# A chained transformer kernel on Trainium2: value products of the softmax attention issued for two key steps at a time

## What is computed

```python
def _L1_attn_ref(embedded, Wq, bq, Wk, bk, Wv, bv, gamma, beta):
    B, S, D, H = (2, 256, 128, 16)
    ...
    qk = jnp.einsum('bhqd,bhkd->bhqk', q, k)
    ...
    qk = qk / jnp.float32(np.sqrt(s))
    p = jax.nn.softmax(qk, axis=-1)
    ...
    mask = jnp.triu(jnp.ones((s, s), dtype=p.dtype), k=0)
    p = p * mask
    z = jnp.einsum('bhqk,bhkd->bhqd', p, v)
    ...
    x = embedded + z
```

## Time and profile before

| | us |
|---|---|
| median of 3 runs | 970.51 |
| lowest, highest | 967.36, 974.08 |
| the profiled execution | 969.55 |
| its span in the trace | 967.8 |

### The profile page before, as it was taken

How to read it: one execution, slowest core, us unless ns; L and a number is a source line. 1 busy time by engine, 2 the same in 40 slices (tenths; PEclk the granted TensorE clock), 3 DMA queues, 4 the chain that set the end, 5 groups by cost and what they waited for, 6 DMA issues and landing times.

```text
span 967.8 us, 13758 instructions
## 1 busy us (share of the span) xinstructions
PE 676.5 (70%) x4446; PEld 336.2 (35%) x4446; DVE 567.8 (59%) x1037; ACT 443.9 (46%) x836; POOL 297.6 (31%) x679
## 2 busy tenths in 40 slices
PE   4052767704315956299999999999899999830793
PEld 4041322503315953013333333332233333230693
DVE  5215599631621447596777777778976876062243
ACT  2031500203103634127877676766767777620562
POOL 0606166051542430022323223230323233105242
PEclk9995799657556986659999999998999999955797
DMA  9952000003202021730030203030100000001203
GB/s 227 245 187 44 1 1 0 1 25 94 39 31 81 27 59 33 176 73 1 2 51 3 49 2 51 2 51 2 33 18 2 1 3 1 2 0 39 78 29 95
DMA packets 45926, 44.89 MB, mean 46 GB/s; under 512 B 5904, under 2 KB 36316, under 8 KB 45600
## 3 DMA queue, kind: packets, MB, share of 16 engines
q1 hardware_dynamic: 41168, 35.90, 16.2%
q0 software_dynamic: 4544, 7.60, 2.9%
q10 hardware_dynamic: 144, 0.51, 0.2%
HBM read 27.85 MB, written 17.60 MB: 47 GB/s over the span
## 4 chain that ended last, share of the span: by engine, by line
PE 56%; DVE 16%; issue 8%; POOL 7%; DMA 7%; ACT 4%; SPq 1%; POOLq 0%; DVEq 0%; ACTq 0%
PE PS L855 14%; PE PS L822 12%; PE PS L797 11%; PE PS L636 5%; PE PS L647 5%; POOL slots_x L1432 4%; DVE ARENA L1385 3%; POOL ARENA L1446 2%; PE PS L543 2%; DVE ARENA L1344 2%; ACT ARENA L1017 2%; DVE XN L1072 2%; DMA ARENA<-slots_x 2%; DVE STATS L1049 1%; DVE PS L1335 1%
## 5 line engine op out<-in xcount | busy, mean ns | idle before, releaser
L1385 DVE TENSOR_REDUCE ARENA<-PS 128x1 f32<-128x1024 f32 x256 | 303.0, 1220 | 94.2 <-PE PS L797 93.7
L1017 ACT ACTIVATE ARENA<-PS 128x512 f32<-128x512 f32 x512 | 279.5, 597 | 95.6 <-PE PS L822 89.2
L822 PE MATMUL PS<-ARENA 75*128 75x512 bf16 x512 | 174.9, 388 | 8.3 <-ACT ARENA L1017 6.8
L797 PE MATMUL PS<-ARENA 72*128 72x512 bf16 x512 | 164.3, 405 | 21.3 <-DMA ARENA<-k_parts 16.9
L855 PE MATMUL PS<-ARENA 128*8 128x128 f32 (+8 forms) x1920 | 153.4, 435 | 0.7 <-ACT ARENA L1017 0.7
L1498 POOL TENSOR_SCALAR_AFFINE_SELECT ARENA<-ARENA 128x128 f32<-128x128 f32 x256 | 74.1, 293 | 161.2 <-ACT ARENA L1017 160.9
L588 PE MATMUL PS<-C,ARENA 128*128 128x128 f32 x78 | 17.0, 372 | 119.4 <-DMA ARENA<-slots_x 119.3
L1302 DVE TENSOR_TENSOR ARENA<-PS,ARENA 128x512 f32<-128x512 f32 x46 | 31.8, 692 | 95.8 <-PE PS L636 95.8
L561 PE MATMUL PS<-C,XN 128*128 128x128 f32 x96 | 25.5, 420 | 89.1 <-DVE XN L1072 88.0
L822 PEld LDWEIGHTS PS<-ARENA 75*128 75x128 bf16 x512 | 47.5, 98 | 105.5 <-ACT ARENA L1017 56.8
L797 PEld LDWEIGHTS PS<-ARENA 72*128 72x128 bf16 x512 | 44.8, 100 | 104.0 <-issue 37.2
(11 more groups left out here) (135 smaller groups left out, 812.4 us busy)
## 6 DMA issues: line engine op xcount, KB each, us to landing
ARENA<-q_parts SPq DMA_DIRECT2D x24, 192.0 KB
ARENA<-k_parts SPq DMA_DIRECT2D x72, 64.0 KB
ARENA<-pack_dram SPq DMA_DIRECT2D x8, 514.0 KB, 16.4
slots_x<-FILL SPq DMA_DIRECT2D x2, 1483.5 KB, 22.3
ARENA<-slots_x SPq DMA_DIRECT2D x10, 258.0 KB, 4.1
ARENA<-slots_x SPq DMA_DIRECT2D x8, 256.0 KB, 3.6
slots_y<-ARENA SPq DMA_DIRECT2D x16, 128.0 KB, 1.8
ARENA<-tokens_y SPq DMA_DIRECT2D x8, 256.0 KB, 4.1
```

Of the source, the lines that this page charges most:

```text
L797: ins = nc.tensor.matmul(PS[:, slot + c, :], Q3[0:KQ, G % Q3R, g, i * P:(i + 1) * P], K3[0:KQ, G % Q3R, g, c * 512:(c + 1) * 512], start=T ...
L822: nc.tensor.matmul(PS[:, bank, 0:w], K3[0:MR + 3, G % Q3R, i, j * P:(j + 1) * P], Q3[0:MR + 3, G % Q3R, i, half * 512:half * 512 + w], sta ...
L1017: nc.scalar.activation(PT[:, n % NPT, 0:w], PS[:, 4 + ring_number[x] % NBB, 0:w], ACT.Exp).then_inc(b_exp, 1)
L1385: nc.vector.tensor_reduce(NM[:, k % 4, i:i + 1], PS[:, slot:slot + 2, :].rearrange("p b n -> p (b n)"), AX.X, ALU.max, negate=True).then_i ...
```

## The change

Two V are issued together behind the third B of every even step: V of step m-2 and V of step m-1. Every M that falls due is held back and comes right behind such a pair, or behind the third B of an odd step, or ahead of the first B of a half. Two more pieces of the list stand ahead of the first step (`LEAD` 2 for 0), and the spread of A, S and M ends 12 steps before the end (`AEND`) where it ended 8 before. The last two V stand together at the end. The engines' own code is unchanged.

```diff
-LEAD = 0
-VD = 1
+LEAD = 2
 VG = 2
+AEND = 12
...
-    plan, at = [], 0
+    plan, at, held = [], 0, []
+
+    def turned():
+
+        plan.extend(held)
+        held.clear()
+
...
         for g in range(4):
-            want = ahead + -(-rest * (4 * m + g + 1) // (4 * (steps - TB)))
+            want = ahead + -(-rest * (4 * m + g + 1) // (4 * (steps - AEND)))
             if g == 0 and s in (0, TB):
 
                 want = max(want, turns.index(("M", 4 * G + 3, s // TB)) + 1 + LEAD)
             while at < min(want, len(turns)):
-                plan.append(turns[at])
+                (held if turns[at][0] == "M" else plan).append(turns[at])
                 at += 1
+            if g == 0 and s in (0, TB):
+                turned()
             plan.append(("B", m, g))
-            if m >= VD and g == VG:
-                plan.append(("V", m - VD, 0))
-                if (m - VD + 1) % (2 * NS) == 0:
-                    plan += [("T", (m - VD) // (2 * NS), 0), ("T", (m - VD) // (2 * NS), 1)]
+            if m >= 2 and m % 2 == 0 and g == VG:
+                plan += [("V", m - 2, 0), ("V", m - 1, 0)]
+                turned()
+                if m % (2 * NS) == 0:
+                    plan += [("T", m // (2 * NS) - 1, 0), ("T", m // (2 * NS) - 1, 1)]
+            elif g == VG:
+                turned()
         plan += [("Z", piece, 0) for piece in range(len(ZSTEPS)) if ZSTEPS[piece] == m]
-    assert at == len(turns)
-    for m in range(steps - VD, steps):
+    assert at == len(turns) and not held
+    for m in range(steps - 2, steps):
         plan.append(("V", m, 0))
```

## The result

| | before | after |
|---|---|---|
| median | 969.23 us (4 runs) | 995.29 us (4 runs) |
| lowest, highest | 967.36, 974.08 | 988.15, 1002.79 |
| profiled execution | 969.55 | 997.24 |
| its span | 967.8 | 995.5 |

The changed kernel takes 1.0253 times as long, with a 95% interval of 1.0216 to 1.0290: 26 us slower. The prediction said 976.5, in a range of 961 to 990.

What follows compares the result with a forecast made beforehand. TensorE bounds the kernel before; after, VectorE's reductions through two score slots decide between pairs. Block terms of +4.3, -1.1, +6.9, -1.8, +0.7 and -2.1 sum to +6.9 on 969.55: 976.5 us, range 961 to 990.

Steps and rivals of the forecast that it cites:

- that rival: Between the two V of a pair: an entry and exit are paid as before, +14.5 us, 991 in all; chance 0.11.
- The chain of two slots: Between pairs of V: A waits for VectorE's reductions to free two score slots; the fourth A starts at a + 3.06 us.
- a and n: Between pairs: a is the first A's delay behind VV (0 to 0.43 us), n the B behind the fourth A (1 to 3).
- the pairing's own gain: At the seam of two V: entry 0.10 and exit 0.13 us are saved once per pair, 0.23 in all.
- One sign: Over the stage: TensorE's idle time ahead of A, ended by VectorE's reductions, comes to some 10 to 20 us.
- segments: Stretches between one VV and the next, with 8 B and 4 A: a + 3.6 + 0.21 n, 3.8 to 4.4 us.
- the ring: Three banks through which B waits for exponentials: 4.1 us at most per stretch between pairs, so rarely last to finish.
- the tail's term: Steps 116 to the last V: no A left, four pairs of 5.17 us, 26.0 in all, -2.1.
- The rival: In the tail: idle time drops the clock to the 1.2 GHz level, a pair takes 7.3 us, +10.6, 987; chance 0.11.
- The start: Up to the first V, one step of B and two A more, +4.3 us; steps 0 to 3, -1.1.
- The other term of the change: Turning behind V: M costs 0.04 us there; elsewhere mostly 0.25, or 0.64 at a few places.
- The 0.64 of a badly placed M: M away from V takes one of three ring banks and B waits: a step of 3.46 us for 2.82.

Runs made afterwards that it cites:

- filler: The changed kernel with a second, unused product ahead of each B from the last B of step 116 on: 988.0 us, 7.3 less than the changed kernel.

## Why the prediction was wrong

**The prices of TensorE at full clock were right.** V is 0.98 and a pair 1.84 to the next B (1.83 was said), with masked columns 2.30 (2.31). The seam is free; that rival is out. By the Trainium skill, TensorEngine Tiling (Array Packing), section Key Properties, a drain belongs to a change of mode and not of tile; the trace agrees: the second V of a pair adds 0.86, the 0.85 that the prediction took for its streaming.

**The chain of two slots was right in the first part,** in place and in size: steps 4 to 67 came out at +5.9 for +6.9, VectorE's gap is 1.28 to 1.74 per two steps between 500 and 530 us (1.3 to 1.8 was said), and putting A at other places moved two steps by the 0.3 us that a and n give. It is the reason that the pairing's own gain, 0.23 a pair, is not seen: TensorE waits for it. One sign came out smaller: TensorE's waits for VectorE's reductions sum to 9.3 us over the stage by the profile, where 10 to 20 were said and before had 3.5. In steps 84 to 107 the segments were mis-sized: 4.16 us (6.00 - 1.84) where 3.95 was said, about 2.5 us over the 12 pairs. There halved reductions hardly help, so the ring, held for "rarely last", is probably as late.

**The step that failed is the tail's term,** "four pairs of 5.17", and with it the chance of 0.11 for the clock. It had the tail's clock stay at 1.00, as it does in the kernel before; but it was about 0.5 during the V of every pair from step 114 to 125. Four pairs took 6.88 us on average for 5.17, and the whole block 34.5 for 26.0: 8.5 of the 20.7 us by which the profiled execution (997.2) lies above 976.5. The rival had the mechanism, the place and nearly the price (7.3 for a tail pair, +10.6 in all), but it was held for unlikely because of steps around 605 us, with a wait in every second step at full clock. That was the wrong row to compare with: there TensorE stands idle for 0.64 us in two steps, in the paired tail for about 1.6 (an estimate: 5.22 at full clock, less 1.84, 8 x 0.21 and 0.10). It also began earlier than the block it was counted in: the last A is issued at 819.02, ahead of the third B of step 114, and the V of steps 114 and 115 already take 4.43 us for 2.30. Taken against the pairs at full clock (5.22 and, masked, 4.18, from the run with pairs only), the low clock costs 4 x 1.66 + 1.7 + 2.1 = 10.4 us in the tail. Single products from step 112 on give back 12.3 us by the medians and 14.0 by the traces, the clock and the pairing's own cost together; filler gives back 7.3 and 6.0, although it comes too late for the first slow V and is work itself. The Trainium skill, TensorE: Matmul & The Clock Gate, section "A second HAM failure mode: psum-queue depth-cycling", describes such a swing between the levels through small idles; the trace agrees, with a granted clock of 0.51 and 1.00 within the same two steps.

**The start was mis-sized:** +5.8 up to step 4, where +3.2 was said. The prediction counted what is moved ahead of the first V (4.3, measured 5.5), but took the pairs behind it at full clock; the first takes 3.64 us to the next B for 2.30. The clock does not fall here, it rises later: it is 0.50 up to the first V in both kernels, and rises during the first V, which now come 7.5 us later. Single products for the first eight steps bring some 2 us back.

**The other term of the change was underrated.** The prediction gave the turning behind V and the constants next to nothing. Turning alone is 6.7 us faster, with the constants 11.4 us, and the constants without it are 11.5 us slower. The 0.64 of a badly placed M was known, but not that the slope of the spread decides how many steps have it. Another 2 us of the miss are chance: the earlier stages were that much slower in the profiled execution.

So the 26 us are the pairing's 36 less the 11 that the rest of the change brings with single products. Where the pairing costs is read best from the traces of two kernels that differ in it alone (times in us; a mark is the fourth B of a step):

| stretch | changed kernel | without pairing | difference |
|---|---|---|---|
| first A to step 10 | 63.9 | 60.6 | 3.4 |
| to step 66 | 182.9 | 174.5 | 8.3 |
| to step 86, beside the normalization | 76.1 | 68.2 | 7.9 |
| to step 112 | 85.0 | 80.9 | 4.2 |
| to the last V | 54.1 | 40.1 | 14.0 |
| outside of these | | | 3.0 |

Together 40.7 for these two executions, against 36 by the medians; the 3.0 outside are chance, and the third row varies by some 4 us between executions of one list. So 12.5 us are the two slots and the ring in the middle, 14.0 the tail, with about 10.4 of it for the clock, and the rest the start and the normalization, both with the low clock in part. Putting A at the best places took 8.7 of the 12.5 back.

## What to carry to other kernels

Joining two blocks of work on one engine saves its seams only if the buffers of the others last through the joined block: work out how long they go without a new tile, and when the first one behind it is ready. Where the joining gathers TensorE's waits in one place, the clock can fall there and nearly double the price of the very block that was joined (3.51 us for 1.84); here the last steps, which have no A between, showed it most. And where several edits come together, take them one at a time: here a harmful one hid a good one, which brings 11 us without it. To compare two orders of one list, measure between instructions up to which both have done the same work.

## What was not expected of the hardware

In the paired tail the clock fell and came back within each pair of steps: V at 3.51 us for 1.84 with a granted clock of 0.51, and the B behind it at 1.00. Adding 45 useless matmuls of 0.21 us made the kernel 7.3 us faster by the medians, and its tail 6.0 us shorter by the traces. And in the run with pairs only, two pairs of the same instructions, one right behind the other, were at either level: 6.51 us and then 5.22.
